# A decoder on one core: first layer's context stage written out, its router products inside it, and the second layer's dense experts fed one slot ahead

## The reference, cut to what matters

```python
# layer 0, cross-attention: query = layernorm(x), batches of 32 queries against 64 context rows
attn = leaky_relu(einsum('bsd,bqd->bsq', context, query), 0.1)
attn = attn / (sqrt(sum(attn * attn, over q) + 1e-8) + 1e-8)
a = softmax(swapaxes(attn, 1, 2) * 9)
cat = concatenate([query, einsum('bqs,bsd->bqd', a, context)])
h, g = tanh(cat @ W_lin + b_lin), sigmoid(cat @ W_gate + b_gate)
x = x + query * g + h * (1 - g)
# layer 0, experts
xn = layernorm(x) * ln_gamma + ln_beta
top 2 of 8 of softmax(xn @ router_w), then those experts and a shared one, added to x
# layer 1, experts: 8 of width 64, all computed, weighted by the shares of the top 2
h = silu(xt @ wg) * (xt @ wu);  x = x + sum over experts of share * (h @ wd) + shared expert
```

## Time and profile before

| | us |
|---|---|
| median of the runs (3) | 1780.94 |
| lowest, highest | 1779.66, 1781.64 |
| the profiled execution's own time | 1782.44 |
| its span, first to last instruction | 1780.7 |
| mean granted TensorE clock | 0.945 |
| PE, DVE, ACT, POOL busy | 1525.0, 1180.0, 984.2, 494.0 |

### The profile page before, as it was taken

The page is one execution under the profiler, slowest core; times in us unless marked ns, Lnnn a source line. Parts: engine busy times, 40 slices in busy tenths (PEclk is TensorE's granted clock), DMA queues, the critical chain, the costliest instruction groups (busy, mean ns, idle before and its releaser), DMA issues. The chain is left out here.

```text
span 1780.7 us, 38657 instructions
## 1 busy us (share of the span) xinstructions
PE 1525.0 (86%) x11095; PEld 1087.3 (61%) x11143; DVE 1180.0 (66%) x3776; ACT 984.2 (55%) x2547; POOL 494.0 (28%) x744
## 2 busy tenths in 40 slices
PE   7999999999999566469999678999999688978776
PEld 4777777777776444248888545555556344545665
DVE  5767776777675595746666457777777379963444
ACT  5767776777676233116666446666666345541332
POOL 3222222323232246333233222222222122310222
PEclk9999999999999796679999979999999899987999
DMA  6000000000000301001111200000000000000000
GB/s 202 1 0 0 0 0 0 0 0 0 0 0 1 142 1 48 1 15 42 44 44 41 64 11 13 12 12 12 12 12 6 1 1 1 0 0 1 12 18 18
DMA packets 34213, 35.04 MB, mean 20 GB/s; under 512 B 5744, under 2 KB 29808, under 8 KB 33392
## 3 DMA queue, kind: packets, MB, share of 16 engines
q1 hardware_dynamic: 29808, 25.48, 4.4%
q0 software_dynamic: 4352, 8.92, 2.0%
HBM read 25.47 MB, written 8.91 MB: 19 GB/s over the span
## 5 line engine op out<-in xcount | busy, mean ns | idle before, releaser
L556 POOL TENSOR_SCALAR a_prob<-a_prob,a_inv 128x128 f32<-128x128 f32 (+1 forms) x256 | 127.0, 507 | 387.6 <-DVE a_inv L468 387.6
L414 ACT ACTIVATE a_prob<-a_psS,a_low 128x128 f32<-128x128 f32 (+1 forms) x512 | 210.5, 438 | 0.5 <-DVE a_low L458 0.5
L458 DVE CUSTOM_DVE_ANT_0 a_psS<-a_psS,a_bias 128x128 f32<-128x128 f32 (+1 forms) x512 | 167.6, 389 | 56.2 <-PE a_psS L295 39.6
L1550 ACT ACTIVATE a_probT<-a_psZ 128x512 f32<-128x512 f32 x256 | 138.9, 594 | 74.2 <-PE a_psZ L1362 74.2
L405 ACT COPY a_probT<-a_psT 128x384 f32<-128x384 f32 x256 | 123.5, 482 | 96.3 <-PE a_psT L336 94.1
L1623 DVE TENSOR_REDUCE a_low<-a_psS 128x4 f32<-128x1024 f32 x128 | 156.2, 1221 | 25.7 <-PE a_psS L1362 24.5
L336 PE MATMUL a_psT<-ident,a_prob 128*128 128x128 f32 x768 | 133.2, 282 | 2.8 <-ACT a_probT L405 2.7
L336 PEld LDWEIGHTS a_psT<-ident,a_prob 128*128 128x128 f32 x768 | 88.0, 140 | 60.2 <-issue 48.6
L295 PE MATMUL a_psS<-a_qk 64*128 64x128 f32 (+1 forms) x1024 | 119.7, 352 | 1.4 <-ACT a_qk L397 0.9
L414 ACT ACTIVATION_READ_ACCUMULATOR a_prob<-a_psS,a_low 128x1 f32 x512 | 113.8, 222 | 0.0
L1156 POOL DMA_INDIRECT e_rows<-rows_dram,source x72 | 68.3, 949 | 160.7 <-PE e_psX L1190 136.8
(11 more groups left out here) (300 smaller groups left out, 3916.0 us busy)
## 6 DMA issues: line engine op xcount, KB each, us to landing
sorted_out<-e_y SPq DMA_DIRECT2D x72, 64.0 KB, 1.5
in_lo<-in_gate_up SPq DMA_DIRECT2D x4, 1024.0 KB, 8.0
x<-in_x SPq DMA_DIRECT2D x8, 256.0 KB, 6.9
down<-in_down SPq DMA_DIRECT2D x1, 2048.0 KB, 16.3
rows_dram<-rows SPq DMA_DIRECT2D x8, 256.0 KB, 3.6
out<-x SPq DMA_DIRECT2D x8, 256.0 KB, 2.3
e_rows<-rows_dram,source POOLq DMA_INDIRECT x72, 2.7
a_sel_in<-in_sel SPq DMA_DIRECT2D x1, 1024.0 KB, 5.0
```

The lines of the kernel that those rows point to most:

```text
L414: nc.scalar.activation(prob[:, 2 * (p % 4) + k, lo:hi], psS[:, u, lo:hi], ACT.Exp, bias=low[:, u, i:i + 1], scale=-1.0, accum_out=total[:, ...
L458: nc.vector.tensor_tensor_reduce(psS[:, u, lo:hi], psS[:, u, lo:hi], bias0[:, 2 * p + k, lo:hi], 1.0, LEAST, ALU.add, ALU.min, low[:, u, i ...
L556: nc.gpsimd.tensor_scalar(w, w, inv[:, 2 * (q % 2) + 1, i:i + 1], 1.0, ALU.mult, ALU.mult).then_inc(norm_done[1], 1)
L1550: nc.scalar.activation(probT[:, (p + half + 1) % 2, 2 * half + c, :, :].rearrange("p j s -> p (j s)"), psZ[:, c, :], ACT.Exp, scale=-1.0). ...
```

## The change

In the context stage the eight units and their three trailing slots are written out for each engine with constant addresses. The turned context is multiplied by the second weight half once per unit (`cw`, bias added on keeping), and the exponents are multiplied with that, so the weighted rows are neither scaled, turned nor kept; the sums come from products with a column of ones, and the scaling by their reciprocal stands in the last multiply-add, onto the kept first half in `pre`. Scores and products read `xnT` directly. ACT makes 0.1 times the scores and the square. POOL makes `diff` and `x_hid` = x + hid in a row, and also `length`. DVE finishes x in the second multiply-add and writes the normalised rows once, to `rows`. Each unit's rows are stored as soon as they stand, and each unit's router products run in the context stage, into a tile that the routing stage reads. The routing stage loses its router products, the copy of them, and its stores. The bias tile is a quarter as wide. In `layer1_experts` `cols_hi` and `cols_lo` are made for slot n+1 at the head of slot n, with a first one ahead of the loop; the last round is written out as well.

```diff
@@ layer0_context: tiles
         psX = ph.ps("psX", [P, 512])
-        psW = ph.ps("psW", [P, 2, 512])
-        psV = ph.ps("psV", [P, 512])
-        psC = ph.ps("psC", [P, UB, 2 * D])
-        psN = ph.ps("psN", [P, 2, 512])
-        q_cur = ph.sb("q_cur", [P, 4, UQ])
-        ctxT_cur = ph.sb("ctxT_cur", [P, 2, 2 * L])
-        ctx1_cur = ph.sb("ctx1_cur", [P, 2, D + 1])
-        tenth = ph.sb("tenth", [P, S])
+        psW = ph.ps("psW", [P, 512])
+        psQ = ph.ps("psQ", [P, UB, 2 * D])
+        psE = ph.ps("psE", [P, UB, 2 * D])
+        psN = ph.ps("psN", [P, 512])
...
@@ layer0_context: SP queue
+            for u in range(UNITS):
+                sp.wait_ge(rows_done, (u + 1) * UB)
+                sp.dma_start(g.rows_dram[cols(u), :].rearrange("(t p) d -> p t d", p=P), g.rows[:, rows(u), :]).then_inc(rows_out, 16)
             sp.wait_ge(experts_in, 16 * 5)
+            sp.wait_ge(rows_out, 16 * UNITS)
@@ layer0_context: PE queue (the lines removed are in the code above)
+            pe.wait_ge(ctxT_ready, 1)
+            pe.wait_ge(ones_set, 1)
+            def scores(u):
+                if u:
+                    pe.wait_ge(leaky_done, u)
+                for j in range(2):
+                    mm = pe.matmul(psX[j * L:(j + 1) * L, 0:S], g.ctxT[:, (2 * u + j) * L:(2 * u + j + 1) * L],
+                                   g.xnT[:, (2 * u + j) * S:(2 * u + j + 1) * S], start=True, stop=True)
+                mm.then_inc(x_scores, 1)
+            def project(u):
+                if u:
+                    pe.wait_ge(cw_kept, u)
+                pe.matmul(psW[:, 0:2 * D], g.ctxT[:, 2 * u * L:2 * (u + 1) * L], g.wcat[:, 1, :], start=True, stop=True).then_inc(cw_done, 1)
+            def mix(u):
+                for k in range(UB):
+                    if u and k % 2 == 0:
+                        pe.wait_ge(q_kept, 2 * (u - 1) + k // 2 + 1)
+                    at = slice(u * UQ + k * P, u * UQ + (k + 1) * P)
+                    pe.matmul(psQ[:, k, :], g.xnT[:, at], g.wcat[:, 0, :], start=True, stop=True).then_inc(q_done, 1)
+                pe.wait_ge(e_done, 2 * u + 2)
+                if u:
+                    pe.wait_ge(invz_done, u)
+                for k in range(UB):
+                    mm = pe.matmul(psL[:, NT * E + k:NT * E + k + 1], e_bd[:, u % 2, k * P:(k + 1) * P], ones[:], start=True, stop=True)
+                mm.then_inc(z_done, 1)
+                pe.wait_ge(cw_kept, u + 1)
+                for k in range(UB):
+                    if u and k % 2 == 0:
+                        pe.wait_ge(pre_done, UB * (u - 1) + k + 2)
+                    pe.matmul(psE[:, k, :], e_bd[:, u % 2, k * P:(k + 1) * P], cw[:, u % 2, :], start=True, stop=True).then_inc(c_done, 1)
...
+            def logits(u, s):
+                pe.wait_ge(kept, u + 1)
+                pe.wait_ge(invz_done, min(s, UNITS))
+                for k in range(UB):
+                    t = UB * u + k
+                    mm = pe.matmul(psL[:, t * E:(t + 1) * E], g.xnT[:, t * P:(t + 1) * P], g.router[:], start=True, stop=True)
+                mm.then_inc(logits_done, 1)
+            for s in range(UNITS + 3):
+                if s < UNITS:
+                    scores(s)
+                    project(s)
+                if s >= 3:
+                    turn(s - 3)
+                if 1 <= s <= UNITS:
+                    mix(s - 1)
+                if s >= 3:
+                    logits(s - 3, s)
@@ layer0_context: ACT queue
+            def tenths(u):
+                act.wait_ge(x_scores, u + 1)
+                if u:
+                    act.wait_ge(leaky_done, u)
+                nc.scalar.mul(tenth[:], psX[:, 0:S], 0.1).then_inc(tenth_done, 1)
...
+            def squares(u):
+                act.wait_ge(leaky_done, u + 1)
+                if u:
+                    act.wait_ge(norm2e_done, u)
+                nc.scalar.activation(square[:], leaky[:, u % 2, :], ACT.Square, accum_out=norm2[:]).then_inc(square_done, 1)
...
+            def tanhs(u):
+                act.wait_ge(pre_done, UB * (u + 1))
+                if u:
+                    act.wait_ge(x_hid_done, u)
+                    act.wait_ge(diff_done, u)
+                nc.scalar.activation(hid[:], pre[:, :, 0:D], ACT.Tanh).then_inc(hid_done, 1)
+                if u:
+                    act.wait_ge(part_done, u)
+                nc.scalar.activation(gate[:], pre[:, :, D:2 * D], ACT.Tanh, scale=0.5).then_inc(gate_done, 1)
...
+            for s in range(UNITS + 3):
+                if s < UNITS:
+                    tenths(s)
+                    squares(s)
+                if s >= 3:
+                    keep(s - 3)
+                if s < UNITS:
+                    exps(s)
+                if 1 <= s <= UNITS:
+                    keep_q(s - 1)
+                    tanhs(s - 1)
+            act.wait_ge(logits_done, UNITS)
+            nc.scalar.copy(g.logits[:].rearrange("p t e -> p (t e)"), psL[:, 0:NT * E]).then_inc(logits_kept, 1)
+            act.wait_ge(logits_kept, 1)
@@ layer0_context: POOL queue
+            def apart(u):
+                pool.wait_ge(hid_done, u + 1)
+                if u:
+                    pool.wait_ge(part_done, u)
+                nc.gpsimd.tensor_tensor(diff[:], g.rows[:, rows(u), :], hid[:], ALU.subtract).then_inc(diff_done, 1)
+                if u:
+                    pool.wait_ge(x_done, u)
+                nc.gpsimd.tensor_tensor(x_hid[:], g.x[:, rows(u), :], hid[:], ALU.add).then_inc(x_hid_done, 1)
+            def lengths(u):
+                pool.wait_ge(square_done, u + 1)
+                nc.gpsimd.tensor_scalar(norm2e[:], norm2[:], 1.0, EPS, ALU.mult, ALU.add).then_inc(norm2e_done, 1)
+                pool.wait_ge(norm2e_done, u + 1)
+                nc.gpsimd.tensor_tensor(root[:], norm2e[:], half[:], ALU.pow).then_inc(root_done, 1)
+                pool.wait_ge(root_done, u + 1)
+                if u:
+                    pool.wait_ge(sharp_done, u)
+                nc.gpsimd.tensor_scalar(length[:], root[:], 1.0 / SMOOTH, EPS / SMOOTH, ALU.mult, ALU.add).then_inc(length_done, 1)
...
+            for s in range(UNITS + 2):
+                if s >= 2:
+                    apart(s - 2)
+                if s < UNITS:
+                    lengths(s)
+                if s >= 2:
+                    rstds(s - 2)
@@ layer0_context: DVE queue
...
+            def update(u):
+                dve.wait_ge(gate_done, u + 1)
+                dve.wait_ge(diff_done, u + 1)
+                v.scalar_tensor_tensor(out=part[:], in0=gate[:], scalar=1.0, in1=diff[:], op0=ALU.add, op1=ALU.mult).then_inc(part_done, 1)
...
+            def weigh(u):
+                dve.wait_ge(z_done, u + 1)
+                if u:
+                    dve.wait_ge(pre_done, UB * u)
+                v.reciprocal(invz[:], psL[:, NT * E:NT * E + UB]).then_inc(invz_done, 1)
+                dve.wait_ge(invz_done, u + 1)
+                for k in range(UB):
+                    dve.wait_ge(q_kept, 2 * u + k // 2 + 1)
+                    dve.wait_ge(c_done, UB * u + k // 2 * 2 + 2)
+                    v.scalar_tensor_tensor(out=pre[:, k, :], in0=psE[:, k, :], scalar=invz[:, k:k + 1], in1=pre[:, k, :], op0=ALU.mult,
+                                           op1=ALU.add).then_inc(pre_done, 1)
...
+            for s in range(UNITS + 2):
+                if s < UNITS:
+                    leakies(s)
+                    keep_cw(s)
+                if s >= 2:
+                    update(s - 2)
+                if s < UNITS:
+                    sharps(s)
+                if s >= 2:
+                    add(s - 2)
+                    stats(s - 2)
+                    aggregate(s - 2)
+                if 1 <= s <= UNITS:
+                    weigh(s - 1)
+                if s >= 2:
+                    apply(s - 2)
@@ Routing.choose, layer0_route_and_shared
+        if psum is not None:
+            self.then(dve, v.tensor_copy(self.logits[:], psum))
-    WHEN = {4: 0, 8: 1, 12: 2, 19: 3, 24: 4}
+    WHEN = {3: 0, 7: 1, 11: 2, 18: 3, 23: 4}
-            for t in range(NT):
-                mm = pe.matmul(psL[:, t * E:(t + 1) * E], g.xnT[:, t * P:(t + 1) * P], g.router[:], start=True, stop=True)
-            mm.then_inc(logits_done, 1)
...
@@ layer1_experts
-                if new:
-                    if lagging:
-                        act.wait_ge(in_done, n - 1)
-                    nc.scalar.copy(cols_hi[:, p % 2, :], g.xnT[:, bass.ds(n * P, P)]).then_inc(cols_ready, 1)
+            def split_hi(n, p):
+                nc.scalar.copy(cols_hi[:, p % 2, :], g.xnT[:, bass.ds(n * P, P)]).then_inc(cols_ready, 1)
+            split_hi(0, 0)
+            def slot(n, p, new, lagging, prep):
+                if prep:
+                    if p or lagging:
+                        act.wait_ge(in_done, n)
+                    split_hi(n + 1, p + 1)
+            def split_lo(n, p):
+                dve.wait_ge(cols_ready, n + 1)
```

(69 more changed lines are left out.)

284 lines of the change are left out of this document (75 added, 209 removed).

## The result

The kernel after the change takes **1730.79 us**, median of 4 runs (1728.19 to 1735.23), beside 1780.30 us for the kernel before in as many (1779.16 to 1781.64). The ratio is 0.9718, with a 95% interval from 0.9703 to 0.9733. The forecast of 1731 holds, but two of its three terms are off in opposite ways. The profiled execution of after is the longest of the four: 1735.23 us, span 1733.4, so 4.4 us above the median.

A forecast was written before the change was run, and what follows sets the result against it. It took DVE as the context's bound, router products as delaying routing, and a PE, DVE, blocked DVE, PE loop as binding the dense experts. Gains 33 + 12 + 5 = 50 off 1780.9 gave 1731 us, range 1719 to 1743.

The forecast's parts named there:

- Dense experts: 33 predicted: Second layer's dense experts: `cols_lo` leaves PE's path, slots go from 3.93 to 2.90 us; gain 33 us, 28.5 to 35.
- Context: 12 predicted: Context stage: units go from 10.66 to 9.2 us, stage ends at 679.2; gain 12 us, 7.6 to 16.6.
- PE's loop ... is next, not late: Context stage: PE's loop takes about 8.4 us a unit at full clock, under the 9.2 us unit.
- The chain from W to W: Context unit, from one unit's last multiply-add to the next's, through tanh, POOL's steps, update and statistics: 8.7 to 9.7 us.
- both new waits: PE's queue in the context: turning waits for normalised rows, router products for DVE's reciprocal; both inside the unit's loop.
- PE at 1.2 GHz in the context: Rival, context stage: PE's loop doubles to 9.6 us, units some 13 us; total 1746 to 1759 us; chance 0.08.
- Routing: 5 predicted: Start of routing: 13.79 us of router products go, but DVE's choice of experts waits for POOL's pieces; gain 5 us.
- From there on the same instructions run: Routing, from the second maximum of the expert choice on: instructions unchanged, no further gain or loss counted.
- The square needs no table load: Context, ACT; the rival claimed the square needs another table, two loads a unit, 9 us in all, 1740 us; chance 0.06.
- Dense experts stay: Rival, second layer's dense experts: `hid` holds `cols_lo` long enough to push `wide`, no gain there; 1764 us; chance 0.05.
- 1.2 GHz in dense experts: Rival, dense experts: PE working without pause is granted 1.2 GHz, slots 5.65 us; all of it gives 1816 us; chance 0.02.
- POOL doesn't get in DVE's way: Rival, choice of experts in routing: DVE is not held by POOL; gain 14.5 instead of 5, 1721 us; chance 0.07.

The follow-up runs named there:

- four more subtractions: Kernel after the change, with `cols_lo` computed four more times into a spare tile in each dense expert: 1731.73 us (ratio 0.9719).
- queries first: Kernel after the change, with PE's four products of the kept rows (the queries) put ahead of the turning of the finished rows: 1719.75 us (0.9655).
- small pieces: Kernel after the change, with ACT's casts and POOL's subtractions of the expert weights cut into 16 instead of 4: 1722.38 us (0.9676).

## Why the prediction was right, point by point

**Dense experts: 33 predicted, 37.7 measured; the mechanism right, the slot mis-sized.** The start came as worked out: slot 2 began 5.42 us after the first product (predicted 5.4), slot 3 at 8.14 (predicted 7.8). Then 28 slots of 2.71 instead of 2.90 make 28 x 0.19 = 5.3 us. The 2.90 was a middle between a block inside a loop round and the stage's mean of 3.04 us, which I had read as loop ends. No loop end shows in this stage: one step in mid-loop (1668.32 - 1665.61) is 2.71 us and so is the mean of all 31. The first-layer stage's mean contains something else, which I haven't separated. The stated range was also narrower than its own slots: 28 of 2.74 from 1655.9 on end at 1732.6, a gain of 37.3, where 35 was written; the measured 37.7 lies outside 28.5 to 35. The room of `cols_lo`, put at 0.7 us, was at least the 0.8 that four more subtractions use.

**Context: 12 predicted, 5.8 in the profile, 9 in the middle of six; the step that failed is "PE's loop ... is next, not late".** The chain from W to W was right: 8.7 to 9.7 a unit was worked out, 8.65 seen where PE keeps up. With it the stage could gain a little more than the upper bound of 16.6 said: with the queries first it gains 692.7 - 675.0 = 17.7 us. The prediction summed PE's loop at full clock only. It had named both new waits, and even the one ahead of the turning "with the whole mix behind it", but gave it no length. PE is early there, stands still, and is then granted 1.2 GHz, at which its loop, with the queries' products behind the turning, no longer fits: units of 10.24 us on the mean instead of 9.2. The rival "PE at 1.2 GHz in the context" described the state and overpriced it: 15 to 28 us for half of the stage at about 13 us a unit. Measured are units of up to 11.93 us beside short ones, (10.24 - 8.63) x 7 = 11 us. It became part of the result, beside the gains, and didn't exclude them. The prediction's own sign, that the forecast falls if the context's clock drops under 0.8, came true with 0.74, and the total held all the same, because the dense experts gave more than forecast.

**Routing: 5 predicted, 5.9 measured.** Second maximum at 22.9 us after the stage's start (predicted 23.8), three steps each until the end of a POOL piece as forecast, shown by the small pieces. "From there on the same instructions run" was true of the instructions and not of their time: 1.7 us went again with PE at half clock.

**The rivals.** The square needs no table load: none stands between 590 and 680, and it takes 0.42 us on ACT. Where a load does stand, at 694.20, it takes 1.28 us and ACT's next instruction starts 0.01 us behind it, so that the 2.66 us which the prediction names beside it isn't seen here. "Dense experts stay" fell with slots of 2.71 us, "1.2 GHz in dense experts" with a clock of 0.99. "POOL doesn't get in DVE's way" fell with 4.48 and 4.60 us. The multiplications moved to ACT cost the chain nothing that shows: `tenth` takes 0.36 us there, and the short units are as short as the lower end of the sum.

So the total was right to 0.2 us partly by luck: +4.7 in one term and -3 (middle of six profiles) to -6 in another.

## What to carry to other kernels

A bound that is taken away leaves the next engine idle at some point of each round, and here PE paid for its pauses again in the work behind them: sum its loop at both clock levels, and look in its queue for independent work to put ahead of each new wait, so that little stands behind the wait if the clock falls. Where a DVE step that reads two SBUF tiles, or a comparison like `hit`, runs beside POOL, price it by the length of one POOL instruction, and cut the POOL work into small pieces if DVE's chain is what the stage waits for. An operation on the path that doesn't depend on the rest of its round is best made one round earlier; then take what the bounding engine itself issues as the new round, without a margin for ends that no row shows.

## What the runs showed of the hardware

- Useless products made a kernel faster: fourteen in place of the first long pause and five in each later unit took 1730.79 to 1723.39 us, with a granted clock of 1.00 in 600 to 660 in place of 0.68 to 0.81.
- After a pause of 6.72 us the clock of PE stayed at 0.50 through 8 us in which it was busy 3.98 and 4.00 of 4 us, and was 0.88 in the next 4. The same context code ended anywhere between 681.8 and 687.7 us from one execution to another, with a clock over 600 to 680 of 0.79 in the first case and 0.74 in the second.
- The low clock costs only what stands in the chain: with the queries first it was 0.50 from 612 to 622 too, and six of the seven steps between units were 8.7 us or less.
- DVE gets in between two POOL instructions that follow each other without a gap: with POOL at work throughout, two DVE steps took 1.24 and 1.37 us with pieces of 1.27, and 4.48 and 4.60 with pieces of 4.5.
- Back to back, 128-wide subtractions of two SBUF tiles start 0.20 us apart on DVE, though each is recorded as 0.28 long.
